# A decoder on one core: four attentions and the first feed-forward stage in one pipeline

## The reference, cut to what matters

```python
def layer0(x, ctx):
    x = layernorm(x + causal_attention_16_heads(x))            # ATTN0
    x = layernorm(x + grouped_attention_32_8_heads(x, ctx))    # CROSS0, no projections
    M = zeros(65536, 8); M[mask_idx] += softmax(expert_atoms) @ atoms * sigmoid(importance)
    logits = x @ gate_w.T                                      # 8 experts, best 2
    y = x @ W + sum_e w[e] * (x @ M[:, e].reshape(256, 256))   # f0, the first feed-forward
    return layernorm(x + y)

def layer1(x, ctx):
    x = layernorm(x + causal_rope_attention_32_8_heads(x))     # ATTN1
    x = layernorm(x + latent_attention_16_heads(x, ctx))       # CROSS1, causal
    return layernorm(x + experts_32_best_6(x))                 # f1: route, experts, combine
```

## Time and profile before

| | us |
|---|---|
| three runs | 925.07, 929.71, 933.79 |
| median | 929.71 |
| the profiled execution: its time | 931.42 |
| its span, first to last instruction | 929.6 |
| first attention stage and its drain | 39.1 to 269.0 |
| ffn0 | 269.0 to 352.5 |
| second attention stage | 352.5 to 622.3 |
| route, experts | 622.3 to 891.3 |
| combine | 891.3 to 929.6 |

### The profile page before, as it was taken

One profiled execution on the slowest core, in us unless ns is written; L12 is line 12 of the kernel. 1 busy time (PEld: TensorE's weight loads), 2 busy tenths in 40 slices (PEclk: granted clock), 3 DMA queues, 4 the chain that ended last, 5 costly groups with the idle time before them and its releaser, 6 DMA issues. The chain is left out here.

```text
span 929.6 us, 18265 instructions
## 1 busy us (share of the span) xinstructions
PE 768.7 (83%) x6887; PEld 470.8 (51%) x6887; DVE 478.0 (51%) x1239; ACT 304.3 (33%) x703; POOL 213.0 (23%) x267
## 2 busy tenths in 40 slices
PE   4599988777839996999999999869969999999900
PEld 4467765555514443555556666647734444444400
DVE  6745665666326883445545444425943333333337
ACT  0012333444221000133333333323335555555500
POOL 3200121111000001000000000023436666666510
PEclk9999998999658995699999999977989999999965
DMA  9492000000020000000000000019312222222263
GB/s 302 125 291 67 2 3 2 2 3 2 1 91 0 1 0 1 1 1 1 2 2 1 2 1 2 1 46 257 118 40 86 86 86 86 86 87 88 71 218 116
DMA packets 48123, 55.28 MB, mean 59 GB/s; under 512 B 7366, under 2 KB 43174, under 8 KB 47334
## 3 DMA queue, kind: packets, MB, share of 16 engines
q1 hardware_dynamic: 38246, 34.11, 12.4%
q0 software_dynamic: 6656, 16.85, 5.4%
q10 hardware_dynamic: 3136, 3.15, 1.0%
HBM read 41.45 MB, written 12.65 MB: 58 GB/s over the span
## 5 line engine op out<-in xcount | busy, mean ns | idle before, releaser
L609 DVE TENSOR_REDUCE nmf<-bank 128x4 f32<-128x512 f32 x192 | 123.7, 686 | 138.8 <-PE bank L295 138.6
L495 ACT ACTIVATE pt<-bank 128x512 f32<-128x512 f32 x192 | 104.2, 595 | 252.3 <-PE bank L315 252.3
L295 PE MATMUL bank<-kk,qT 32*128 32x256 f32 x768 | 115.5, 419 | 15.2 <-ACT pt L495 8.3
L726 POOL TENSOR_TENSOR rstd<-vare,half 128x1 f32<-128x1 f32 x32 | 17.7, 552 | 438.8 <-DVE vare L670 438.8
L295 PEld LDWEIGHTS bank<-kk,qT 32*128 32x128 f32 x768 | 70.7, 194 | 53.6 <-issue 36.8
L1464 PE MATMUL bank<-wgu,g_xgT 128*64 x256 | 90.6, 477 | 0.0
L1464 PE MATMUL bank<-g_wgu,g_xgT 128*64 128x352 f32 x256 | 90.6, 477 | 0.0
L315 PE MATMUL bank<-nm,sel 32*128 32x128 f32 x768 | 86.4, 343 | 0.0
L307 PE MATMUL bank<-qT,kk 32*128 32x512 f32 x256 | 78.0, 687 | 1.7 <-ACT pt L495 1.4
L1429 POOL DMA_INDIRECT out_rows<-g_og,g_out_row x64 | 63.4, 990 | 58.1 <-DVE g_og L1533 54.9
L1484 PE MATMUL bank<-wd,g_hT 128*64 x256 | 68.9, 392 | 0.1
(11 more groups left out here) (243 smaller groups left out, 1370.5 us busy)
## 6 DMA issues: line engine op xcount, KB each, us to landing
wgu<-in_L_ffn_w_gate SPq DMA_DIRECT2D x4, 1408.0 KB
wgu<-in_L_ffn_w_up SPq DMA_DIRECT2D x4, 1408.0 KB
wd<-in_L_ffn_w_down SPq DMA_DIRECT2D x32, 176.0 KB
g_y<-out_rows SPq DMA_DIRECT2D x4, 768.0 KB, 16.6
g_y<-out_rows ACTq DMA_DIRECT2D x4, 768.0 KB, 17.2
sparse_table<-f_m_re SPq DMA_DIRECT2D x2, 1024.0 KB
f_m_re<-sparse_table SPq DMA_DIRECT2D x2, 1024.0 KB
f_idx_row<-in_L_ffn_mask_idx SPq DMA_DIRECT2D x1, 1024.0 KB
```

Source lines behind the costliest of these rows:

```text
L295: return pe.matmul(bank, q, k, start=first, stop=r == 1, skip_group_check=True)
L495: act.activation(T.pt[2 * (t % 2) + u][:, :], STB[u][:, :], ACT.Exp, scale=own[v].scale).then_inc(exp_done, 1)
L609: dve.tensor_reduce(T.nmf[v % 2][:, 2 * (c % 2) + u, at:at + 4], SB[u][:, :].rearrange("p (h k) -> p h k", h=4), AX.X, ALU.max, negate=Tru ...
```

## The change

One call of `attention` takes all four attentions, V = 32, and holds ffn0. Units get a place in the list of hosts: units 0 to 15 at places 0 to 15, units 16 to 31 at 20 to 35; the hosts 16 to 19 between them have four steps each and hold two feed-forward tiles each, tile t in the steps c = 2 (t mod 2) and the next. The hosts 17 to 19 are at the same time the three that fill the pipeline for unit 16. The two hosts at the end that drain have four steps instead of two.

- The four pair banks become the two STB banks, and the base and the transposed x share bank M. A pair waits until the pair two before it was added.
- The table is scattered two parts per host, w from 0 to 7; SP waits for all 16 and reads it back while the first attention runs. Both copies into the layout are VectorE's, in host 15.
- `f_m` gets a place of its own, `f_m_re` shares its with the small tiles of ffn0 and rope. ffn0 has its own statistics tiles.
- `base` of tile 0 is in the last step of host 15. `norm` of tile t - 1 now stands behind `choose(t)`, both at the head of tile t's first step.
- The two casts of line 700 and 701 stand at the end of all four attentions. One barrier and one set of memsets of the value tiles go, with one stage's end.

```diff
+    place = [v if v < FFN_AT else v + FFN_HOSTS for v in range(V)]
+    at_place = {p: v for v, p in enumerate(place)}
     def hosted(w):
-        return max([n[v] for v in (w, w + 1) if has(v)] or [n[0] if w < 0 else n[-1]])
+        return max([n[unit(p)] for p in (w, w + 1) if p in at_place] or [n[0] if w < 0 else 4])
+    def tile_of(w, c):
+        return 2 * (w - FFN_AT) + c // 2 if FFN_AT <= w < FFN_AT + FFN_HOSTS else None
...
+            sp.wait_ge(placed, NS // 128 * 16)
+            for j in range(KT):
+                sp.dma_start(F.m_re[:, j, :], F.table[j * 128 * 256:(j + 1) * 128 * 256, :]
+                             .rearrange("(p r) e -> p (r e)", p=128)).then_inc(table_back, 16)
...
                     if i == 0:
                         pe.wait_ge(nm_copied, v + 1)
+                        if v == FFN_AT:
+                            pe.wait_ge(added, B * E0)
...
+            def ffn_transpose(t):
+                pe.wait_ge(ln_done, B + t + 1)
+                if t > 0:
+                    pe.wait_ge(base_used, t)
+                for j in range(KT):
+                    last = pe.transpose(M[:, j * 128:(j + 1) * 128], T.x_all[:, t, j * 128:(j + 1) * 128], T.ident[:])
+                last.then_inc(f_xt_done, 1)
+            def ffn_pair(t, q):
+                p = 4 * t + q
+                if p == 0:
+                    pe.wait_ge(exp_done, 2 * before[FFN_AT])
+                    pe.wait_ge(m_ready, 2)
+                if p >= 2:
+                    pe.wait_ge(added, 2 * (p - 1))
+                for j in range(KT):
+                    last = pe.matmul(STB[q % 2][:, :], F.xT[t % 2][:, j * 128:(j + 1) * 128], F.m[:, j, 2 * q:2 * q + 2, :],
+                                     start=(j == 0), stop=(j == KT - 1))
+                last.then_inc(pair_done, 1)
+            def ffn(w, c):
+                t = tile_of(w, c)
+                if w == FFN_AT - 1 and c == 2:
+                    ffn_transpose(0)
+                elif w == FFN_AT - 1 and c == 3:
+                    ffn_base(0)
+                elif t is not None and c % 2 == 0:
+                    ffn_pair(t, 0)
+                    ffn_pair(t, 1)
+                    ffn_transpose(t + 1)
+                elif t is not None:
+                    ffn_pair(t, 2)
+                    ffn_base(t + 1)
+                    ffn_pair(t, 3)
...
             for w, c, count in hosts:
                 exponentials(t_pair(w, c))
+                ffn(w, c)
...
+            def ffn(w, c):
+                t = tile_of(w, c)
+                if w == FFN_AT - 1 and c in (1, 2):
+                    dve.wait_ge(table_back, 16 * KT)
+                    j = c - 1
+                    dve.tensor_copy(F.m[:, j, :, :], F.m_re[:, j, :].rearrange("p (r e) -> p e r", e=E0)).then_inc(m_ready, 1)
+                elif t is not None and c % 2 == 0:
+                    choose(t)
+                    if t > 0:
+                        ffn_norm(t - 1)
+                    ffn_start(t)
+                    for e in range(E0 // 2):
+                        ffn_add(t, e)
+                elif t is not None:
+                    for e in range(E0 // 2, E0):
+                        ffn_add(t, e)
+                    ffn_stats(t)
+                elif w == FFN_AT + FFN_HOSTS and c == 0:
+                    ffn_norm(B - 1)
...
                 if c == 0:
-                    stage_qk(w + 3)
-                    place_entries(w)
+                    stage_qk(unit(w + 3))
+                    place_entries(2 * w)
+                if c == 1:
+                    place_entries(2 * w + 1)
...
-        if "x0" in STAGES:
-            attention(nc, (ATTN0, CROSS0), T, F)
-        if "f0" in STAGES:
-            ffn0(nc, T, F, banks)
-        if "x1" in STAGES:
-            attention(nc, (ATTN1, CROSS1), T, F)
+        attention(nc, (ATTN0, CROSS0, ATTN1, CROSS1), T, F)
```

More of the change, by code:

```diff
@@ L133, in attention @@
     biased = lambda cfg: cfg.bias
-    hosts = [(w, c, hosted(w)) for w in range(-3, V + 2) for c in range(hosted(w))]
-    with Stage(nc, first_cfg.name) as stage, ExitStack() as ctx:
+    hosts = [(w, c, hosted(w)) for w in range(-3, place[-1] + 3) for c in range(hosted(w))]
+    with Stage(nc, "at") as stage, ExitStack() as ctx:
         sem = stage.sem
@@ L181, in s_pair @@
         def s_pair(w, c):
-            nxt, soon = w + 1, w + 2
+            nxt, soon = unit(w + 1), unit(w + 2)
             if c == hosted(w) - 1 and has(soon):
@@ L190, in t_pair @@
         def t_pair(w, c):
-            return (w, c) if has(w) and c < n[w] else None
+            v = unit(w)
+            return (v, c) if has(v) and c < n[v] else None
         def previous(w, c):
@@ L540, in _ @@
+                    copy_xt(unit(w + 3))
         @block.vector
@@ L680, in _ @@
                 if c == count - 2:
-                    split_maxima(w + 1)
+                    split_maxima(unit(w + 1))
                 if c == 0:
[L683 to L686, removed]
+                    norm(unit(w - 2))
+                    rope(unit(w + 2))
+                    queries(unit(w + 2))
+                    keys(unit(w + 2), True)
                 if count == 2 and c == 0:
-                    keys(w + 2, False)
-                    value_rows(w + 2)
-                    normalise(w - 1)
+                    keys(unit(w + 2), False)
+                    value_rows(unit(w + 2))
+                    normalise(unit(w - 1))
                 if count == 4 and c == 1:
-                    normalise(w - 1)
-                    keys(w + 2, False)
-                    value_rows(w + 2)
+                    normalise(unit(w - 1))
+                    keys(unit(w + 2), False)
+                    value_rows(unit(w + 2))
                 if c == count - 1:
[L696 to L701, removed]
+                    residual(unit(w - 1))
+                ffn(w, c)
+            dve.tensor_copy(T.before_bf[:], T.before[:])
+            dve.tensor_copy(T.columns_bf[:], T.columns[:])
         @block.gpsimd
@@ L728, in place_entries @@
             def place_entries(t):
-                if not (has(t) and first_cfg is ATTN0):
+                if not 0 <= t < NS // 128:
                     return
@@ L740, in _ @@
             pool.wait_ge(v_cleared, 6)
[L741 removed]
+            wide_cfg, narrow_cfg = ATTN0, CROSS0
             for i in range(3):
```

351 lines of the change are left out of this document (158 added, 193 removed).

## The result

On the chip of the prediction the changed kernel took 899.9 us, the median of five runs (899.54 to 909.14), beside 928.73 us for the kernel before (923.92 to 933.79): a ratio of 0.9709, 95% interval 0.9666 to 0.9752. The profiled execution is the slowest of the five, 909.14 us with a span of 907.4 (the other four have spans of 897.7 to 898.7), so its rows add up to less gain than the median shows: 22.2 us of span.

A forecast was written before the change was run, and what follows sets the result against it. Waits and half clock between the attention stages' steady parts (142.3 us), VectorE slightly slower than TensorE in the tiles; 22.9 + 1.3 - 0.4 = 23.8 us off 931.42 gives 907.6, or 906 by the median; range 898 to 917.

The forecast's parts named there:

- the sum of gains: Whole execution: 22.9 us up to unit 16's first transposed fill, 1.3 for that fill, less 0.4 for casts: 23.8 us.
- Early table: Sparse table's read-back near 155 us, 100 us before needed, under the first attention; the 7.4 us wait comes back.
- Two copies on VectorE, and two scatters per host, at no cost: First attention: copies of 2 x 2.01 us fit host 15's idle VectorE; paired scatters cost nothing, at worst 3 us.
- base(0) ending at 263.8: Seam before the first feed-forward tile: its base matmuls end at 263.8 us instead of 282.73.
- Tile 0: First feed-forward tile: pairs at 268.4, 270.5, 273.4 and 276.2, the first at half clock, ending at 278.3 us.
- The plain tile of 10.8: Feed-forward tiles with two pair banks: a chain between VectorE and TensorE takes 10.8 us, 2.5 more than 8.25 before.
- rival 3: Tiles and ramp: engines overlap better than the chain, logits 8.3 us apart, 43 us saved, 888 us; chance 0.06.
- I take full clock from tile 1: Feed-forward tiles: TensorE, busy 8.0 of 10.8 us, runs at full clock from the second tile on.
- rival 2: Tiles: clock falls for about three, or hops and in-order waits make each 12.5 us; +13 us, 919; chance 0.12.
- Rival 1: Tiles: the clock falls and stays at half, each chain 15.3 us; +34 us, 964, slower; chance 0.05.
- The ramp's tiles: Tiles 4 to 7, holding the third attention's ramp: tiles 4, 5 and 6 take 12.6, 12.1 and 15.6 us.
- The last add at 362.0: End of tile 7: its last add at 362.0 us releases unit 16's first transposed fill, at 384.86 before.

The follow-up runs named there:

- e2: The changed kernel with the table's read-back held until unit 15's last exponential: 926.12 us (920.57 without the four highest runs), ratio 0.9823 to the kernel before.
- e6: The changed kernel, still with two banks, with base(t+1) moved behind the tile's fourth pair: 910.48 us, ratio 0.9685 to the kernel before.
- e4: The changed kernel with four pair banks in tiles 0 to 4 and all four pairs ahead of the next transposes: 908.29 us, ratio 0.9658 to the kernel before.
- e10: The changed kernel unaltered, run again on the chip of e8 and e9: 904.9 us, ratio 0.9771 to the kernel before.
- e1: The changed kernel unaltered, run again on another chip: 917.02 us (915.12 without the highest run), ratio 0.9786 to the kernel before.
- e3: The changed kernel with units 16 to 31 three hosts later, so the third attention's ramp stands behind the tiles: 935.85 us, ratio 0.9979 to the kernel before.
- e5: The changed kernel with five added matmuls on idle data in each step of host 15 and host 14's last: 906.78 us, ratio 0.9654 to the kernel before.
- e8: e4 with pair 3 ahead of base(t+1) in tiles 5 to 7: 899.71 us, ratio 0.9696 to the kernel before.
- e9: e8 with the added matmuls of e5: 894.02 us, ratio 0.9645 to the kernel before.
- e7: The kernel before, unaltered, run once more for a second profile: 937.82 us (one run).

## Why the prediction was right, and where its sizes were off

The forecast of 906 us held the sign, the range (898 to 917) held the time, and the chain of reasons held; the sum of gains came out at 27.7 us from root to root and 28.8 in the medians, against 23.8. By its steps:

- **Early table: right.** The read-back went out at 149.21 (forecast near 145), 104 us ahead of its use. For its price I gave 7.4 us and part of the copies' 3.9; e2 puts it at 9.1 or 5.4 by the medians and 13 to 15 in its profile, so the size is neither confirmed nor refuted.
- **Two copies on VectorE, and two scatters per host, at no cost: right.** The copies lie in host 15 (252.96 to 256.93); they push unit 14's residual behind them, and VectorE still idles 5.93 us before the first logits. From unit 0's root to unit 12's it takes 150.3 us, 149.9 before.
- **base(0) ending at 263.8: it ended at 265.1,** with the first attention 3.2 late. From unit 12's root it is 1.9 us earlier than forecast, with a clock that fell at 247 instead of at 241.
- **Tile 0: too long.** I had four pairs, the first at half clock, end at 278.3; it ended at 277.41, 12.3 us behind base(0) instead of 14.5.
- **The plain tile of 10.8: right,** 10.62 in the trace, and e6 (9.73) and e4 (8.26) show its terms one by one. The share of rival 3, logits 8.3 apart, needed the banks that the change took away.
- **"I take full clock from tile 1": failed in part.** It fell twice, for 1.5 and 1.7 us in tiles 1 and 2 (12.16 and 12.64 from one tile's statistics to the next, forecast 10.8 and 11.2). This was rival 2 in kind, at a quarter of its price. Rival 1, half clock to the end, did not come: after each fall the pairs that follow ran without breaks and the clock was full again within 4 us.
- **The ramp's tiles: each a little shorter.** Tile 4 took 12.0 us for 12.6, tile 5 11.7 for 12.1, tile 6 14.7 for 15.6 and was the longest, as forecast. Each is counted from the end of one tile's statistics to the next. The fills lie in TensorE's 1.65 us waits more than I had them.
- **The last add at 362.0: at 361.65,** and the first mask_kq fill at 361.75. The errors cancel to 0.3 us: the late start and the dips against tile 0, the late clock fall and the ramp.
- **Why the median gained more than 23.8.** The sum took one execution's seam as the kernel's. Seams of before were 189.1 and 182.0 us, those of the changed kernel 161.35, 160.3 and 155.6 (first profile, e10, e1). The gain is 20.7 to 33.5 us by which are paired; the medians show 28.8, 22.1 (23.8 without the highest runs) and 21.8 on chips A, B and D. The forecast's 23.8 lies within what the chips give, and its 906 was high by 6.1 on the chip it was made for. That the sum came so near is in part luck, since one more profile of the kernel before moves the seam it starts from by 7 us. What set that chip's other four runs some 9 us below the profiled one was not profiled and stays open; their clocks (0.947 to 0.949, against 0.937) point to fewer falls, which no profile of them shows.

On the clock the Trainium skill, page "TensorE: Matmul & The Clock Gate", section "A second HAM failure mode: psum-queue depth-cycling", holds that cycling through PSUM banks with pauses sends the clock back and forth. In the traces here it went to half in tiles 1 and 2 of four profiles (the first, e2, e3, e10) and in e2's tile 5, and in none of the tiles behind tile 0 in e1, e5 and e6, which cycle the same two banks. So a clock that goes back and forth exists in this kernel, at 0 to 5.1 us. The prediction had put the section beside rival 1, the clock at half to the end; what it describes is nearer to rival 2, and that is what came in part.

## What to carry to other kernels

Joining two stages pays for the ramp that it hides, and only if the order of the shared queue doesn't cost as much: here the overlap gave some 19 us and the two-bank tiles took 19. When stages share PSUM banks, write down the chain from one engine's instruction to the other's over one tile before the instruction counts: it gave 10.8 where busy times gave 8.25, and it named both repairs (banks that the neighbour leaves idle, and nothing between the matmuls that the other engine waits for). Anchor profiles at a unit's own instruction before you subtract them, and profile the same kernel twice before you take a stall at half clock as its property.

## What the hardware did that I had not expected

- **The clock's fall moves between executions of one kernel.** In the same drain it fell at 241 or only at 258 us (kernel before), and at 246 to 247 or only behind 250 (changed kernel: the first profile and e10, then e1). That is worth 2 to 7 us and is as large as the effects of e5 and e6. In the tiles the same waits of 1.65 us dropped it in some executions and in others not. With the four-bank tiles of e4, e8 and e9 it kept full until tile 5, which then took 15.98, 17.63 and 17.62 us (14.32 in e1). In e9 a wait of 2.00 us ahead of the transposes stands beside its fall:

```profile
308.00:316.00 8.00, 6.00 (x19) 2.89 (x18) 5.55 (x19) 0.97 (x3) 0.27 (x1) 0.71 0.01 3
...
310.71 0.41 PE L461 MATMUL bank<-ident,x_all 128*128 128x128 f32 x2 [2.00 <-DVE f_acc L836]
```

- **Chips differ in a part that no edit touched.** From the last root to the end, the profiles show 308.6 to 310.8 us on chips A and D and 316.8 to 321.5 on B and C, for both kernels. The down projections of the experts (line 1527 of the changed kernel, start of the first to start of the last) took 189.8 us on A (first fence) and 199.0 on B, in e1 (second fence):

```profile
L1527 PE MATMUL bank<-wd,g_hT x256: 379/379/430, 672.8 to 862.6; 128*64 x128
```

```profile
L1527 PE MATMUL bank<-wd,g_hT x256: 379/379/689, 664.3 to 863.3; 128*64 x128
```

  The median matmul is the same 379 ns. The longest is 689 there and 430 here, but that is not what tells the chips apart: on C the kernel before took 200.8 us with a longest of 431 (e7). What makes the stretch longer stays open. Its 10 us are most of what the medians of the kernel before differ by from chip to chip (926.7 and 928.7 against 939.1 and 939.6).
